# Pointwise product and threshold statistics in one stage, and depthwise convolution on square TensorE tiles

## What is computed

```python
h = x + _conv(x, p['blk_cpe_w'][l], p['blk_cpe_b'][l], 3, groups=C)   # depthwise, 7x7
h = _bn(_pw(h, p['blk_fc1_w'][l], p['blk_fc1_b'][l]), ...)            # 64x64 product per pixel
xj = _mr_xj(h, K)
```

```python
xr0 = jnp.roll(x, (H // 2, W // 2), axis=(2, 3))
norm = jnp.sum(jnp.abs(x - xr0), axis=1, keepdims=True)
thr = jnp.mean(norm) - jnp.std(norm, ddof=1)        # per image
```

## Time and profile before

| | |
|---|---|
| Median of 3 runs | 8505.98 us (8499.84 to 8510.32) |
| The profiled execution | 8487.06 us |
| Its span in the profile | 8485.2 us, mean granted TensorE clock 0.902 |
| Busy: TensorE, VectorE, ScalarE, GpSimd | 71%, 60%, 51%, 38% of the span |
| DMA | 841.70 MB, mean 99 GB/s |

### The profile page before, as it was taken

The page is one execution under the profiler, slowest core; times in us unless marked ns, Lnnn a source line. Parts: engine busy times, 40 slices in busy tenths (PEclk is TensorE's granted clock), DMA queues, the critical chain, the costliest instruction groups (busy, mean ns, idle before and its releaser), DMA issues. The chain is left out here.

```text
span 8485.2 us, 82873 instructions
## 1 busy us (share of the span) xinstructions
PE 5984.2 (71%) x26092; PEld 2959.6 (35%) x26286; DVE 5096.2 (60%) x5868; ACT 4346.2 (51%) x4790; POOL 3214.9 (38%) x1140
## 2 busy tenths in 40 slices
PE   7896577667776676985676432363998849889798
PEld 5673111111111111334111111252886627666263
DVE  2111799899999898650799654224222223459596
ACT  1123699899999898750899311101001121125657
POOL 0161799899999897000898031000000000000000
PEclk9998899999999999998999766586999979999898
DMA  6567330111211101667000322255547879984545
GB/s 124 131 199 238 59 40 20 40 60 21 40 20 25 65 30 35 192 160 145 24 11 1 105 45 50 42 90 157 103 85 126 149 188 170 188 171 126 181 124 186
DMA packets 1476784, 841.70 MB, mean 99 GB/s; under 512 B 638754, under 2 KB 1406264, under 8 KB 1462664
## 3 DMA queue, kind: packets, MB, share of 16 engines
q1 hardware_dynamic: 1261032, 717.18, 36.9%
q10 hardware_dynamic: 215456, 120.95, 6.0%
HBM read 533.33 MB, written 304.65 MB: 99 GB/s over the span
## 5 line engine op out<-in xcount | busy, mean ns | idle before, releaser
L1025 POOL TENSOR_TENSOR ag_D<-ag_X 128x2048 f32<-128x2048 f32 (+15 forms) x940 | 2907.7, 3127 | 1060.9 <-DMA ag_X<-h 941.8
L1089 PE MATMUL ag_slot<-ag_S,ag_w 128*128 128x512 bf16 x4768 | 1470.7, 389 | 838.7 <-DVE ag_J L1131 720.9
L1131 DVE TENSOR_TENSOR ag_J<-ag_J,ag_slot 128x1024 f32<-128x1024 f32 x1240 | 1454.7, 1214 | 153.4 <-PE ag_slot L1089 72.9
L1138 DVE SCALAR_TENSOR_TENSOR ag_J<-ag_slot,ag_J 128x1024 f32<-128x1024 f32 (+14 forms) x1640 | 1436.4, 928 | 0.0
L1056 ACT ACTIVATE ag_slot<-ag_D 128x1024 f32<-128x1024 f32 x1280 | 1308.5, 1025 | 173.8 <-DVE ag_J L1138 58.9
L1040 ACT ACTIVATE ag_A<-ag_D 128x2048 f32<-128x2048 f32 x640 | 1212.1, 1894 | 0.0
L1089 PEld LDWEIGHTS ag_slot<-ag_S,ag_w 128*128 128x128 bf16 x4960 | 286.5, 98 | 2256.7 <-DVE ag_J L1131 1299.8
L1082 PE MATMUL ag_dist<-ag_A,ag_given 128*32 128x512 f32 x5120 | 698.5, 618 | 101.6 <-ACT ag_A L1040 77.6
L255 PE MATMUL dc_ps<-dc_high,dc_w_high 128*128 128x512 f32 (+1 forms) x1056 | 425.2, 403 | 281.2 <-DVE dc_low L68 281.2
L1048 ACT ACTIVATE ag_S<-ag_dist,ag_limit 128x512 bf16<-128x512 f32 x640 | 486.7, 761 | 2.3 <-PE ag_dist L1082 2.3
L269 ACT ACTIVATE dc_out<-dc_ps,shift,scale 128x512 f32<-128x512 f32 (+1 forms) x88 | 67.4, 766 | 818.2 <-PE dc_ps L255 818.2
(11 more groups left out here) (208 smaller groups left out, 9521.9 us busy)
## 6 DMA issues: line engine op xcount, KB each, us to landing
ag_X<-h SPq DMA_DIRECT2D x18, 2048.0 KB, 13.3
xj<-ag_J SPq DMA_DIRECT2D x18, 2048.0 KB, 7.2
c_mul<-gated SPq DMA_DIRECT2D x64, 512.0 KB, 11.5
wa_x<-r SPq DMA_DIRECT2D x128, 256.0 KB, 2.9
u<-wa_x SPq DMA_DIRECT2D x128, 256.0 KB, 2.4
mn_x<-u SPq DMA_DIRECT2D x64, 512.0 KB, 5.7
cpe_band<-in_band SPq DMA_DIRECT2D x16, 1792.0 KB, 8.0
gr_hj<-h SPq DMA_DIRECT2D x168, 128.0 KB, 2.8
```

The lines of the kernel that those rows point to most:

```text
L1025: pool.tensor_tensor(self.tile_part(self.d[u % self.DEPTH][:], u, piece), self.span(g, axis, there, there + hi - lo), self.span(g, axis, l ...
L1089: mm = self.nc.tensor.matmul(self.slot[v % self.SLOTS][:, b, :], self.w[:, weights + 2 * h + b, :], self.s[u % 3][:], start=False, stop=Tr ...
L1131: dve.tensor_tensor(best, best, new, ALU.max).then_inc(self.dve_steps, 1)
L1138: dve.scalar_tensor_tensor(out=best, in0=self.slot_part(v, lo, hi), scalar=-1.0, in1=best, op0=ALU.mult, op1=ALU.max)\
```

## The change

`pointwise` and `threshold` are replaced at all five levels by one stage, `pointwise_threshold`. A unit of work is 512 columns of a pair from the upper half of the image and the 512 columns half an image below (32 units at level 0, 8 at level 1, 2 at the others, there with 512, 128 and 32 columns). Per unit: two products into two PSUM banks, one ScalarE pass over both with scale and bias, two VectorE subtractions of the two halves with columns swapped, directly from SBUF, a ScalarE Abs, a product with ones, and the statistics. Products of unit s stand ahead of the distance product of unit s - 2 on TensorE. SP issues loads and stores, in groups of four units (2 transfers of 1 MB each way at levels 0 and 1). `h1` isn't read back.

`cpe_tiles` replaces `cpe_bands` at level 1 and `cpe_small` at level 2. The array is used as NG = 2 tiles of 64x64 (level 1) or NG = 4 of 32x32 (level 2) along its diagonal; each tile takes its own half or quarter of the channels, with all 4 images as 256 or 128 columns. Everything of the level is kept in SBUF; loads come in BATCH = 4 batches, all issued ahead of the first store. Bands are loaded once and as long rows. Both new stages open with `counted`. On the host, a band matrix is made for level 2 as well.

```diff
+def cpe_tiles(nc, name, src, bands, dst, size):
...
+        rows = lambda g: slice(g * R, (g + 1) * R)
+        of_step = lambda k, g: acc[k % RING][g][rows(g), 0:NW].rearrange("h (m w) -> h m w", w=W)
+        per_batch = 16 * NG * (IMG + 1)
...
+            for t in range(BATCH):
+                for g in range(NG):
+                    at = slice(g * KS + t * KB, g * KS + (t + 1) * KB)
+                    sp.dma_start(band[rows(g), t * KB:(t + 1) * KB], bands[:, at, :, :]).then_inc(loaded[t], 16)
+                    for m in range(IMG):
+                        sp.dma_start(x[rows(g), t * KB:(t + 1) * KB, m, :], s_v[3:R + 3, at, m, :]).then_inc(loaded[t], 16)
+            for t in range(BATCH):
+                sp.wait_ge(added, (t + 1) * KB * NG)
+                for g in range(NG):
+                    at = slice(g * KS + t * KB, g * KS + (t + 1) * KB)
+                    for m in range(IMG):
+                        sp.dma_start(d_v[:, at, m, :], out[rows(g), t * KB:(t + 1) * KB, m, :]).then_inc(stored, 16)
+            sp.wait_ge(stored, 16 * BATCH * NG * IMG)
+        @block.tensor
+        def _(pe):
+            for k in range(KS):
+                if k % KB == 0:
+                    pe.wait_ge(loaded[k // KB], per_batch)
+                reach(pe, added, (k - RING + 1) * NG)
+                for dw in range(7):
+                    for g in range(NG):
+                        mm = nc.tensor.matmul(of_step(k, g), band[rows(g), k, dw, :], x[rows(g), k, :, dw:dw + W],
+                                              start=(dw == 0), stop=(dw == 6))
+                mm.then_inc(summed, 1)
...
+                dve.wait_ge(summed, k + 1)
+                for g in range(NG):
+                    dve.tensor_tensor(out[rows(g), k], of_step(k, g), x[rows(g), k, :, 3:W + 3], ALU.add).then_inc(added, 1)
...
+def pointwise_threshold(nc, n, name, src, weight, dst, size, scale, bias):
...
+            def load(k):
+                g, p = groups[k]
+                reach(sp, summed, (k - IN + 1) * nsub)
+                for e in range(2):
+                    at = e * half + g * cols
+                    sp.dma_start(x[k % IN][:, e], src[p, :, at:at + cols]).then_inc(loaded[k % IN], 16)
+            def store(k):
+                g, p = groups[k]
+                sp.wait_ge(scaled, (k + 1) * nsub)
+                for e in range(2):
+                    at = e * half + g * cols
+                    sp.dma_start(dst[p, :, at:at + cols], h[k % KEEP][:, e]).then_inc(stored[k % KEEP], 16)
+            sp.dma_start(w[:], weight).then_inc(w_loaded, 16)
+            for k in range(min(IN, NK)):
+                load(k)
+            for k in range(NK):
+                store(k)
+                if k + IN < NK:
+                    load(k + IN)
...
+            for s in range(NU + 2):
+                if there(s):
+                    k, j = units[s]
+                    pe.wait_ge(loaded[k % IN], 32 * (k // IN + 1))
+                    reach(pe, scaled, s - 1)
+                    for e in range(2):
+                        mm = nc.tensor.matmul(acc[s % 2][:, e, 0:sub], w[:], x[k % IN][:, e, j * sub:(j + 1) * sub],
+                                              start=True, stop=True)
+                    mm.then_inc(summed, 1)
+                if there(s - 2):
+                    u = s - 2
+                    pe.wait_ge(absed, u + 1)
+                    reach(pe, noted, u - SUMS + 1)
+                    nc.tensor.matmul(dist[u % SUMS][:, 0:sub], n.ones[:], lines(d[u % DIFFS][:]), start=True, stop=True)\
+                      .then_inc(dist_summed, 1)
+        @block.scalar
+        def _(act):
+            for s in range(NU + 1):
+                if there(s):
+                    k, j = units[s]
+                    act.wait_ge(summed, s + 1)
+                    if j == 0:
+                        reach(act, stored[k % KEEP], 32 * (k // KEEP))
+                        reach(act, diffed, 2 * (k - KEEP + 1) * nsub)
+                    act.activation(h[k % KEEP][:, :, j * sub:(j + 1) * sub], acc[s % 2][:, :, 0:sub], ACT.Identity,
+                                   bias=bias, scale=scale).then_inc(scaled, 1)
+                if there(s - 1):
+                    u = s - 1
+                    act.wait_ge(diffed, 2 * (u + 1))
+                    act.activation(d[u % DIFFS][:], d[u % DIFFS][:], ACT.Abs).then_inc(absed, 1)
+            act.wait_ge(step, PAIRS)
+            act.activation(sd[:], mv[:, :, 1], ACT.Sqrt, scale=float(count / (count - 1))).then_inc(step, 1)
+        @block.vector
+        def _(dve):
+            for s in range(NU + 2):
+                if there(s):
+                    k, j = units[s]
+                    dve.wait_ge(scaled, s + 1)
+                    reach(dve, dist_summed, s - DIFFS + 1)
+                    of_half = lambda e: h[k % KEEP][:, e, j * sub:(j + 1) * sub].rearrange("c (r w) -> c r w", w=W)
+                    for x0, x1 in ((0, W // 2), (W // 2, 0)):
+                        dve.tensor_tensor(d[s % DIFFS][:, :, x0:x0 + W // 2], of_half(0)[:, :, x0:x0 + W // 2],
+                                          of_half(1)[:, :, x1:x1 + W // 2], ALU.subtract).then_inc(diffed, 1)
+                if there(s - 2):
+                    u = s - 2
+                    p, at = seen[u]
+                    dve.wait_ge(dist_summed, u + 1)
+                    dve.bn_stats(stats[:, p, at, :], dist[u % SUMS][:, 0:sub]).then_inc(noted, 1)
...
-            if l < 2:
+            if l < 1:
                 cpe_bands(nc, f"cpe{l}_", hx[l], a.band[l], cpe[l], SIZE[l])
+            elif l < 3:
+                cpe_tiles(nc, f"cpe{l}_", hx[l], a.band[l], cpe[l], SIZE[l])
             else:
                 cpe_small(nc, f"cpe{l}_", hx[l], a.cpe_w[l], cpe[l], SIZE[l])
-            pointwise(nc, f"fc1_{l}_", flat(cpe[l]), a.fc1_w[l], flat(h1[l]), SIZE[l] ** 2, col(n.scale, ("fc1", l)), col(n.shift, ("fc1", l)))
-            threshold(nc, n, f"thr{l}_", h1[l], SIZE[l])
+            pointwise_threshold(nc, n, f"fc{l}_", flat(cpe[l]), a.fc1_w[l], flat(h1[l]), SIZE[l], col(n.scale, ("fc1", l)), col(n.shift, ("fc1", l)))
```

More of the change, by code:

```diff
@@ L596, in _ @@
                     mm.then_inc(summed[p], 1)
+def pointwise_threshold(nc, n, name, src, weight, dst, size, scale, bias):
+    W = size
+    half = size * size // 2
+    cols = min(half, 2048)
+    sub = min(cols, BANK)
+    nsub = cols // sub
+    rows = sub // W
+    groups = [(g, p) for g in range(half // cols) for p in range(PAIRS)]
+    units = [(k, j) for k in range(len(groups)) for j in range(nsub)]
+    NK, NU = len(groups), len(units)
+    per_pair = NU // PAIRS
+    IN, KEEP, DIFFS, SUMS = 4, 3, 4, 3
+    count = size * size
+    there = lambda u: 0 <= u < NU
+    with ExitStack() as ctx:
+        sb = lambda nm, shape: ctx.enter_context(nc.sbuf_tensor(name + nm, shape, F32))
+        ring = lambda nm, m, shape: [sb(f"{nm}{k}", shape) for k in range(m)]
+        w = sb("w", [P, P])
+        x = ring("x", IN, [P, 2, cols])
+        h = ring("h", KEEP, [P, 2, cols])
+        d = ring("d", DIFFS, [P, rows, W])
+        stats = sb("stats", [P, PAIRS, per_pair, 6])
+        mv = sb("mv", [P, PAIRS, 2])
+        sd = sb("sd", [P, PAIRS])
+        acc = [ctx.enter_context(nc.psum_tensor(f"{name}acc{k}", [P, 2, BANK], F32)) for k in range(2)]
+        dist = [ctx.enter_context(nc.psum_tensor(f"{name}dist{k}", [P, BANK], F32)) for k in range(SUMS)]
+        v = ctx.enter_context(counted(nc, "w_loaded", "summed", "scaled", "diffed", "absed", "dist_summed", "counted", "thr_steps",
+                                      *[f"loaded_{k}" for k in range(IN)], *[f"stored_{k}" for k in range(KEEP)]))
+        block, w_loaded, summed, scaled, diffed, absed, dist_summed, noted, step = v[:9]
+        loaded, stored = v[9:9 + IN], v[9 + IN:]
+        lines = lambda t: t.rearrange("c r w -> c (r w)")
+        seen = {}
+        for u, (k, j) in enumerate(units):
+            p = groups[k][1]
+            seen[u] = (p, sum(1 for e in range(u) if groups[units[e][0]][1] == p))
+        @block.sync
+        def _(sp):
+            def load(k):
[17 more added lines that the diff above has]
+                    load(k + IN)
+            for k in range(min(KEEP, NK)):
+                sp.wait_ge(stored[k], 32 * ((NK - 1 - k) // KEEP + 1))
+        @block.tensor
+        def _(pe):
+            pe.wait_ge(w_loaded, 16)
+            for s in range(NU + 2):
[30 more added lines that the diff above has]
+            act.activation(sd[:], mv[:, :, 1], ACT.Sqrt, scale=float(count / (count - 1))).then_inc(step, 1)
+        @block.vector
+        def _(dve):
+            for s in range(NU + 2):
[12 more added lines that the diff above has]
+                    dve.bn_stats(stats[:, p, at, :], dist[u % SUMS][:, 0:sub]).then_inc(noted, 1)
+            dve.wait_ge(noted, NU)
+            for p in range(PAIRS):
```

(7 more changed lines are left out.)

25 lines of the change are left out of this document (23 added, 2 removed).

## The result

| | before | changed |
|---|---|---|
| Median (4 runs each) | 8506.99 us | 8205.72 us (8196.83 to 8207.80) |
| The profiled execution | 8487.06 us | 8206.47 us |
| Its span, mean granted clock | 8485.2 us, 0.902 | 8202.8 us, 0.913 |

The ratio of the medians is 0.9642, with an interval from 0.9627 to 0.9657: 301 us faster, where 276 were forecast (8230 us, range 8165 to 8350). The sign, the range and the likeliest case held.

What follows compares the result with a forecast made beforehand. No engine bounds the kernel; each stage waits for the one before. Savings of 96 + 32 + 27 + 81 + 35 + 6 = 277 us from 8487.06 give 8210, plus 18.9 for the median, say 8230 us; range 8165 to 8350.

Steps and rivals of the forecast that it cites:

- likeliest case: Whole kernel: the forecast itself, 8230 us, was given a chance of 65%, ahead of all rivals.
- Fused level 0: Fused pointwise and threshold stage, level 0: TensorE leads, 200.9 us becomes 105, saving 96; bounds 100 and 120.
- 5 us added for interference: Fused stage, level 0: 5 us added because TensorE's and DMA's limits lie near each other and disturb each other.
- levels 2 to 4: Fused stages at the small levels: shorter chain saves 13, 7.5 and 6.5 us, together 27 (17 to 30).
- Depthwise level 1: Depthwise stage, level 1: 208.1 us becomes 127, saving 81 (120 to 145), with products at 0.112 us an instruction.
- Depthwise level 2: Depthwise stage, level 2: SP's issuing sets the time, 130.0 us becomes 95, saving 35 (60 to 125).
- 144 x 0.64 = 92: Depthwise level 2: SP issues 80 loads and 64 stores one after another at 0.64 us each, 92 us.
- Openings: Ahead of the replaced stages: five more stage openings turn to the short kind, saving 6 us (0 to 8).
- Diagonal tiles: Rival, depthwise levels 1 and 2: tiles sharing neither rows nor columns don't run together; kernel at 8360 us; chance 12%.
- short instructions: Rival, depthwise level 2: instructions follow no faster than 0.112 us, stage 117 to 126, kernel 8255 us; chance 14%.
- each product alone: Rival, depthwise levels 1 and 2: weights and columns never overlap, 0.57 us a pair at level 1; 8990 us; chance 3%.
- lockstep: Rival, fused levels 0 and 1: TensorE waits on ScalarE and VectorE at half clock, 182 and 57 us; 8325; chance 5%.

Runs made afterwards that it cites:

- the run with short distances: Changed kernel with the distance product and statistics of each fused unit cut to 128 of 512 columns; 8184.68 us, fused level 0 85.7 us.

## Why the prediction was right, and where it was off

- **Fused level 0 (105 said, 99.3).** Its terms held: start 8.1 (7.9), TensorE 85.4 with the slow start (86.6, from 703.48 to 790.13), tail 6.5 (4.7). The 5 us added for interference were wrong: DMA at 424 GB/s didn't make TensorE wait, not even in the run with short distances, where a unit took 2.01 us.
- **Fused level 1 (38, measured 38.3); levels 2 to 4 (27 saved, measured 27.9).** As said; half of level 2's gain was right for the two smallest.
- **Depthwise level 1 (127, measured 128.1).** Two errors that cancel. Products 99.8 for 100.3 plus 2.5 of slow clock, and the tail 10 as said; but the start of 18.4 in place of 13.5, since the bands, on 64 partitions at a time, were priced at the 400 GB/s of transfers to 128 (over all partitions it was 14.1). That the total came out within 1.1 us is luck.
- **Depthwise level 2 (95, measured 77.3).** The mechanism was right, the size off: the term "144 x 0.64 = 92" measured 144 x 0.52 = 75.4, with 1.9 behind it. The price came from `grapher`'s transfers; here the median issue was 0.43 us, and a few of 1.5 raise the mean. This is the largest miss, 17.7 us on the side of faster, and inside the term's own bounds (60 to 125).
- **Openings (6).** Not seen. The stages ahead of the fused ones took 346.6 us at level 0 (345.3 before), 46.3 at level 3 (46.3) and 25.3 at level 4 (26.3), and the one ahead of depthwise level 2 took 113.0 both times: only one of them is shorter, by 1 us, which is within the spread.
- **Rivals.** Diagonal tiles run together (0.111 us), short instructions follow in 0.035, and each product alone would need 0.57. What the prediction took for a property of the hardware, that different tiles overlap, is also one of the order: with the loops exchanged level 1 gets 100 us slower than before the change. And lockstep is avoided by the distance of two units alone.
- **Sum.** 294 in stages for 277: 17.7 more by depthwise level 2 and 5.6 by fused level 0, less the 6 of openings. Where the other 7 up to the medians' 301 lie is not shown, since the profiled execution of before was 20 us under its median. Part of it can lie in the replaced stages themselves: in the kernel with tiles alone the same old pointwise and threshold stages took 343.9 us, against 337.2 in that profile.

## What to carry to other kernels

Interleave products so that neighbours in the program are in different tiles of the array, and place a dependent product as many units behind its source as the chain between them takes; both orders cost nothing and here were worth 180 and 62 us in single stages. Where a stage of small transfers is left, count the transfers on the queue that issues them: split them over queues, spread them over all partitions, and only then shorten the first load and the last store. When two stages merge, price start and end apart from the rate in the middle.

## What the hardware showed that was not expected

- TensorE, busy without a break, stayed at half its clock for 260 us when one tile of 64x64 after the other was at work, and for 100 us with tiles of 32x32. With two tiles of 64x64 side by side it was granted 1.00, and so it was with the whole array busy for only 85.6 of 140 us.
- Four tiles of 32x32 take an instruction in 0.032 to 0.035 us with the slow start, and in 0.028 behind it. That is shorter than the 62 ns that the Trainium skill, "TensorE: Matmul & The Clock Gate", section "Wait — 56ns, not 53.3ns?", gives as the least spacing where a matmul is decoded in microcode, and that the prediction weighed; it fits the 25 ns given there otherwise.
- DMA moved 424 GB/s, reads and writes together, over 20 us.
- 0.9 MB to 64 partitions held SP for a median of 5.0 us at its issue and 0.45 MB for 0.61; 1.8 MB to 128 partitions held it for 0.66, but the rows behind it then for up to 5.8.
